# Cross-attention of a decoder layer: the next tile's value projection is issued ahead of its query projection

## The chip, the cores and the metric

The kernel runs on one core of one Trainium2 chip. The metric is the device time of one execution in microseconds (us); lower is better. Given for a kernel is the median of several runs.

## The reference: what is computed

A decoder layer over 16 rows of 128 tokens with 256 features: an RWKV mixing layer in both directions, then a cross-attention on a context of 16 x 128 tokens, then a block with causal attention and a mixture of 8 experts whose weights are quantised in groups of 128. A layer norm stands behind each of the three. The change touches the cross-attention alone:

```
H = 16; D_K = 256 // 16
q = split_heads(x @ Wq + bq)
k = split_heads(ctx @ Wk + bk)
v = split_heads(ctx @ Wv + bv)
scores = einsum('bhqd,bhkd->bhqk', q, k) / sqrt(D_K)
p_attn = softmax(scores, axis=-1)
x = merge_heads(einsum('bhqk,bhkd->bhqd', p_attn, v)) @ Wo + bo
x = layernorm(x_before + x)
```

The expert weights need, for each group of 128 numbers, a largest and a smallest value, a scale and a rounding to 16 levels. The kernel does this for 16 "whole" weight jobs, one in each step of the cross-attention, beside it.

## The kernel before

The program has seven stages, one behind the other: prep, mix, cross, attend, route, experts, finish. Each stage gives each engine its list of instructions, written out by hand; an engine works off its own list in order, and semaphores hold it where it needs another's result. Nothing reorders instructions.

The cross stage (`cross_stage`) has 16 steps, one for each tile n of 128 tokens (step 0 by itself, steps 1 to 12 in a loop of pairs, steps 13 to 15 written out). It is a software pipeline over three tiles. In step n, TensorE (PE) does:

- `scores(j, 1, n)`: the scores of the second half of the heads (L940); `turn_heads` of tile n-1 (L972); `turn_probs(0, n)` (L950); `join` of tile n-1, the output projection (L981), into the PSUM bank `V`
- `front(n+1)`: the transposition of the next tile's x (L913), its keys (L919), its queries (L924, which wait for ScalarE's copy of the turned x, semaphore `x_t_ready`), and its values (L931)
- then four rounds of transposing the quantised weights (`turn_whole`, L993) with the sums over probabilities (`sums`, L962), `turn_probs(1, n)` and `scores(0, n+1)` between them.

The bank `V` is shared by `join` of tile n-1 and by the values of tile n+1. So the values' matmuls wait for `joined_read` (and `v_read`): VectorE (DVE) must have taken the joined rows of tile n-1 out of the bank (`join_stats`, L1202).

DVE does in step n, in this order: `clip` (L1226, waits for `rounded` of ScalarE), `peaks(1, n)` (L1186 and L1189), `steps_of` (L256 to L261), `join_stats(n-1)` (L1202, L752 to L757), `take_values(n+1)` (L1179, waits for `v_ready`), `range_of` (L240, L241), `peaks(0, n+1)`, `normalise(n)` (L1194, L1196), `join_norm(n-1)` (L1209).

ScalarE (ACT) does: `back(n-1)` (L1065), `collect(0, n)` (L1060), `soften(1, n)` (L1055), `take_x(n+1)` (L1041), `round_part` 0 (L1075, two of the weight tiles), `take_qk(n+1)` (L1046 and L1049, waits for `qk_ready` behind the queries), then `take_whole` and `round_part` in turn (L1085, L1075) with `collect(1, n)` between them, until `rounded` and `soften(0, n+1)`.

GpSimd (POOL) builds the whole weights behind the clip (L1151) and spreads the keys (L1133). SyncE's queue loads each weight job and each tile's rows two steps ahead.

Of the kernel before, what the change touches and what calls it, by code (L numbers as in the profile page):

```python
# [27 lines left out]
B, S, D = 16, 128, 256  # L28
TOK = B * S
DC = D // P  # L30
# [729 lines left out]
def cross_stage(k):  # L760
# [8 lines left out]
    nc, t, banks = k.nc, k.t, k.banks  # L769
# [40 lines left out]
    v_ready = k.semaphore("v_ready")  # L810
    v_read = k.semaphore("v_read")
# [19 lines left out]
    TURN, QK, V, SCORES, PROBS_T, HEADS = 0, 1, 2, 3, 5, 7  # L831

    joined_read = k.semaphore("joined_read")
# [67 lines left out]
    def tensor(pe):  # L901
# [5 lines left out]
        def front(j, n, i, begin=False):  # L907

            pe.wait_ge(rows_in[j], 32 * i + 32)
            if not begin:  # L910
                pe.wait_ge(heads_t_ready, n)
            for c in range(DC):
                last = pe.transpose(banks[:, TURN, c * P:(c + 1) * P], x_in[j][:, c * P:(c + 1) * P], k.ident)  # L913
            last.then_inc(x_turned, 1)
            if not begin:
                pe.wait_ge(qk_read, n)
            for m in range(DC):
                for c in range(DC):
                    pe.matmul(banks[:, QK, (DC + m) * P:(DC + m + 1) * P], wk[:, c, m * P:(m + 1) * P],  # L919
                              ctx_t[j][:, c, :], start=(c == 0), stop=(c == DC - 1))  # L920
            pe.wait_ge(x_t_ready, n + 1)
            for m in range(DC):
                for c in range(DC):
                    last = pe.matmul(banks[:, QK, m * P:(m + 1) * P], wq[:, c, m * P:(m + 1) * P],  # L924
                                     x_t[j][:, c, :], start=(c == 0), stop=(c == DC - 1))
            last.then_inc(qk_ready, 1)
            if not begin:
                pe.wait_ge(v_read, n)
                pe.wait_ge(joined_read, n)
            for c in range(DC):  # L930
                last = pe.matmul(banks[:, V, 0:D], ctx_t[j][:, c, :], wv[:, c, :], start=(c == 0), stop=(c == DC - 1))  # L931
            last.then_inc(v_ready, 1)

        def scores(j, h, n, begin=False):
            pe.wait_ge(spread_ready, 2 * n + h + 1)
# [61 lines left out]
        def step(j, n, i, prev, more):  # L997
            def tiles(r):
                turn_whole(j, n, r, min(more, 1))

            scores(j, 1, n)
            if prev:
                turn_heads(1 - j, n - 1, 1)
            turn_probs(0, n)
            if prev:
                join(1 - j, n - 1, 1)
            if more:
                front(1 - j, n + 1, i + 1)
            else:
                pe.wait_ge(qk_read, B)  # L1010
                k.open_attend("pe", pe)
            tiles(0)
            sums(j, 0, n)
            tiles(1)
            turn_probs(1, n)
            if more:
                scores(1 - j, 0, n + 1)
            else:
                pe.wait_ge(scores_read, 2 * B)
                k.open_attend("pe", pe)  # L1020
            tiles(2)
            sums(j, 1, n)
            tiles(3)
            if not more:
                k.open_attend("pe", pe)

        front(0, 0, 0, True)
        scores(0, 0, 0, True)
        in_steps(step, pe)
# [1540 lines left out]
```

## Time and profile before

| what | us |
|---|---|
| median of 3 runs | 1191.3 (1191.14 to 1192.22) |
| the profiled execution, its own time | 1189.91 |
| its span, first to last instruction | 1188.2 |
| cross stage within the span | about 274 to 515 |

A row of the timeline gives the start in us from the span's start, the time taken, the engine, the line, the operation, the tile written and read, and how many instructions are merged in it; in brackets stands the idle time ahead of it and what ended that. Matmuls are pipelined: the next may start before the last one's end. One fp32 matmul of the program is two or more in the trace.

### The profile page before, as it was taken

What the parts mean: (1) busy time and instruction counts of PE and PEld (TensorE: products, weight loads), DVE (VectorE), ACT (ScalarE), POOL (GpSimd) and SP (SyncE); (2) the same over time, 40 slices, a digit from 0 to 9 for tenths busy, and PEclk for the clock granted to TensorE, in tenths of its full rate; (3) what the DMA queues carried; (4) which work ended last, traced back from release to release, by engine and by line L of the source; (5) the groups of instructions that cost most, each with busy time, mean ns of one, the idle gap of its engine ahead of it and who ended that gap; (6) DMA issues with size and microseconds to landing.
All of it is one profiled execution on the core that took longest, in us unless ns stands there. A gap on an engine that the chain in (4) does not pass through costs nothing.

```text
span 1188.2 us, 24715 instructions
## 1 busy us (share of the span) xinstructions
PE 968.9 (82%) x7366; PEld 744.4 (63%) x7367; DVE 959.0 (81%) x2172; ACT 752.0 (63%) x1885; POOL 601.8 (51%) x639
## 2 busy tenths in 40 slices
PE   0495877535999989968999999993799999999991
PEld 0342433324777777745666666662799999999990
DVE  6859999997888888876999998866577777777773
ACT  4864444304888888844666777651477777777773
POOL 2859776853444444421557667751544444434333
PEclk9897988867998899988999999996899999999995
DMA  5860010131333333216122112221122222222224
GB/s 192 346 224 3 1 36 1 35 115 59 117 120 120 120 120 120 90 58 249 38 101 71 59 49 72 67 63 38 32 42 44 37 40 40 39 43 38 40 32 151
DMA packets 53493, 96.77 MB, mean 81 GB/s; under 512 B 9840, under 2 KB 41584, under 8 KB 52928
## 3 DMA queue, kind: packets, MB, share of 16 engines
q1 hardware_dynamic: 45328, 83.35, 20.4%
q0 software_dynamic: 8112, 12.78, 6.2%
q8 instruction: 25, 0.41, 0.1%
q14 instruction: 28, 0.23, 0.1%
HBM read 66.37 MB, written 29.74 MB: 81 GB/s over the span
## 4 chain that ended last, share of the span: by engine, by line
PE 43%; DVE 34%; issue 9%; ACT 5%; POOL 4%; DMA 3%; DVEq 0%; SPq 0%; ACTq 0%; POOLq 0%
PE banks L2166 15%; PE banks L2176 10%; DVE mix_sums L685 4%; DVE carry L672 2%; DVE peak L1186 2%; DVE carry L675 2%; PE banks L1452 2%; DVE probs L1189 2%; DVE whole_stat L241 2%; DVE whole_stat L240 2%; PE banks L1430 1%; PE banks L1475 1%; PE banks L1467 1%; ACT whole_level L1075 1%; PE banks L924 1%
## 5 line engine op out<-in xcount | busy, mean ns | idle before, releaser
L2266 DVE SCALAR_TENSOR_TENSOR expert_gate<-banks,expert_steps,expert_chunk 128x128 f32<-128x128 f32 x546 | 164.8, 346 | 76.8 <-ACT expert_chunk L2226 58.2
L2166 PE MATMUL banks<-expert_parts,levels 128*128 128x128 bf16 x3276 | 196.9, 220 | 1.0 <-ACT expert_parts L2221 1.0
L2166 PEld LDWEIGHTS banks<-expert_parts,levels 128*128 x3276 | 189.0, 98 | 6.9 <-issue 1.2
L2230 ACT ACTIVATE silu<-expert_gate,expert_steps 128x128 f32<-128x128 f32 x273 | 109.6, 402 | 77.9 <-DVE expert_gate L2266 76.0
L488 PE MATMUL banks<-x_turned,w_rkv 128*128 128x512 f32 (+1 forms) x192 | 103.1, 698 | 39.4 <-DVE weight L666 35.4
L2176 PE MATMUL banks<-down,up 128*128 x546 | 134.9, 387 | 0.0
L2337 POOL DMA_INDIRECT summed_d<-expert_y,expert_target x39 | 62.5, 1602 | 126.6 <-ACT expert_y L2236 123.5
L2226 ACT COPY expert_chunk<-banks 128x256 f32<-128x256 f32 x273 | 99.8, 366 | 14.5 <-PE banks L2166 12.9
L1151 POOL TENSOR_TENSOR whole<-whole_level,whole_stat 128x896 bf16<-128x896 f32 x32 | 53.2, 1684 | 102.1 <-DVE whole_level L1226 102.1
L2176 PEld LDWEIGHTS banks<-down,up 128*128 128x128 f32 x546 | 97.6, 190 | 10.4 <-issue 0.4
L488 PEld LDWEIGHTS banks<-x_turned,w_rkv 128*128 128x128 f32 x192 | 42.2, 226 | 97.5 <-issue 92.9
L2273 DVE SCALAR_TENSOR_TENSOR up<-expert_gate,expert_steps,silu 128x128 f32<-128x128 f32 x273 | 95.0, 348 | 8.2 <-ACT silu L2230 8.2
L1075 ACT ACTIVATE whole_level<-whole_raw,whole_stat 128x128 f32<-128x128 f32 x224 | 91.2, 486 | 0.2 <-DVE whole_stat L261 0.2
L585 ACT ACTIVATE weight<-weight 128x1024 f32<-128x1024 f32 x16 | 17.0, 1064 | 70.5 <-DVE weight L666 70.4
L962 PE MATMUL banks<-v_ones,probs_t 128*128 128x17 f32 x512 | 61.1, 261 | 0.0
L962 PEld LDWEIGHTS banks<-v_ones,probs_t 128*128 128x128 f32 x512 | 59.7, 192 | 0.0
L1430 PE MATMUL banks<-attend_w,xn_t 128*128 128x512 f32 x128 | 58.7, 601 | 0.0
L1475 PE MATMUL banks<-attend_w,o_turn 128*128 128x256 f32 x256 | 58.1, 380 | 0.5 <-ACT logits L1591 0.5
L2309 POOL DMA_INDIRECT expert_rows<-normed_d,token x39 | 41.2, 1057 | 31.3 <-POOL token L2306 30.5
L1570 ACT ACTIVATE att_probs<-att_probs,low_peak 128x128 f32<-128x128 f32 x128 | 49.5, 390 | 11.4 <-DVE low_peak L1816 11.3
L1699 POOL TENSOR_TENSOR att_probs<-att_probs,att_share 128x1024 f32<-128x1024 f32 x16 | 30.3, 1896 | 49.8 <-DVE att_share L1820 49.8
L685 DVE RECIPROCAL mix_sums<-gate 128x512 f32<-128x512 f32 x16 | 53.6, 3353 | 0.6
(265 smaller groups left out, 2421.4 us busy)
## 6 DMA issues: line engine op xcount, KB each, us to landing
whole_raw<-in_weight_jobs SPq DMA_DIRECT2D x16, 896.0 KB, 5.3
levels_d<-whole_t SPq DMA_DIRECT2D x16, 448.0 KB, 2.8
levels<-levels_d SPq DMA_DIRECT2D x16, 448.0 KB, 3.9
raw<-in_weight_jobs SPq DMA_DIRECT2D x6, 896.0 KB, 4.9
numbers_d<-turned SPq DMA_DIRECT2D x6, 896.0 KB, 7.4
down<-in_weight_jobs SPq DMA_DIRECT2D x5, 896.0 KB, 7.1
normed_d<-normed_parts SPq DMA_DIRECT2D x16, 192.0 KB, 1.9
attend_w<-numbers_d SPq DMA_DIRECT2D x3, 896.0 KB, 6.6
```

The source lines that it names most:

```text
L488: last = pe.matmul(banks[:, 3 * (u % 2) + m, :], w_rkv[:, kc, col:col + P], x_turned[d][:, kc, bass.ds(g * GT, GT)], start=(kc == 0), stop ...
L685: st.did(dve.reciprocal(sums[p][:, 1, :], gate[u][:, :]))
L962: last = pe.matmul(banks[:, HEADS, head * (XK + 1):(head + 1) * (XK + 1)], probs_t[h][:, 4 * m + a, :], v_ones[j][:, head, :], start=True, ...
L1075: last = act.activation(level[j][:, a, :], raw[j][:, a, :], ACT.Identity, bias=stat[j][:, BIAS, a:a + 1], scale=stat[j][:, INV, a:a + 1])
L1430: last = pe.matmul(banks[:, at[m], :], xn_t[:, c, :], w_qkv[:, c, 512 * m:512 * m + 512], start=(c == 0), stop=(c == DC - 1))
L1475: last = pe.matmul(banks[:, TURN, 0:D], o_turn[:, h, :], w_o[:, h, :], start=(h == 0), stop=(h == QH - 1))
L2166: last = pe.matmul(banks[:, at, (m * DC + c) * ROWS:(m * DC + c + 1) * ROWS], levels[:, bass.ds(expert * (2 * JOB) + (m * JOB + (f * DC + ...
L2176: last = pe.matmul(banks[:, Y + j, 0:D], up[j][:, f, :], down[:, bass.ds(expert * JOB + f * D, D)], start=(f == 0), stop=(f == FC - 1))
L2226: act.copy(chunk[slot(j, f)][:, :, :], halves(at)[:, :, 0, :]).then_inc(chunk_ready, 1)
L2230: act.activation(silu[slot(j, f)][:, :], gate[slot(j, f)][:, 0, :], ACT.Silu, scale=steps[j][:, 0, 0, f:f + 1]).then_inc(silu_ready, 1)
L2266: last = dve.scalar_tensor_tensor(out=gate[slot(j, f)][:, m, :], in0=halves(at)[:, m, 1, :], scalar=steps[j][:, m, 1, f:f + 1], in1=chunk[ ...
L2273: dve.scalar_tensor_tensor(out=up[j][:, f, :], in0=gate[slot(j, f)][:, 1, :], scalar=steps[j][:, 1, 0, f:f + 1], in1=silu[slot(j, f)][:, : ...
```

## The change

In `front` the value projection, with its two waits, is put between the key projection and the queries' wait. The instructions and the waits of each are the same, and only PE's list changes.

```diff
                 for c in range(DC):
                     pe.matmul(banks[:, QK, (DC + m) * P:(DC + m + 1) * P], wk[:, c, m * P:(m + 1) * P],
                               ctx_t[j][:, c, :], start=(c == 0), stop=(c == DC - 1))
+            if not begin:
+                pe.wait_ge(v_read, n)
+                pe.wait_ge(joined_read, n)
+            for c in range(DC):
+                last = pe.matmul(banks[:, V, 0:D], ctx_t[j][:, c, :], wv[:, c, :], start=(c == 0), stop=(c == DC - 1))
+            last.then_inc(v_ready, 1)
             pe.wait_ge(x_t_ready, n + 1)
             for m in range(DC):
                 for c in range(DC):
                     last = pe.matmul(banks[:, QK, m * P:(m + 1) * P], wq[:, c, m * P:(m + 1) * P],
                                      x_t[j][:, c, :], start=(c == 0), stop=(c == DC - 1))
             last.then_inc(qk_ready, 1)
-            if not begin:
-                pe.wait_ge(v_read, n)
-                pe.wait_ge(joined_read, n)
-            for c in range(DC):
-                last = pe.matmul(banks[:, V, 0:D], ctx_t[j][:, c, :], wv[:, c, :], start=(c == 0), stop=(c == DC - 1))
-            last.then_inc(v_ready, 1)
```

On PE, inside the loop over steps, `front` from its keys to the first round of turned weights, with - for before and + for now:

```order
 L919 MATMUL banks<-ctx_t,w_k 128x128 [waits qk_read]
 L919 MATMUL banks<-ctx_t,w_k 128x128 x3
-L921 REGISTER_ALU
-L924 MATMUL banks<-x_t,w_q 128x128 [waits x_t_ready]
-L924 MATMUL banks<-x_t,w_q 128x128 x3
-L931 MATMUL banks<-w_v,ctx_t 128x256 [waits joined_read,v_read]
-L931 MATMUL banks<-w_v,ctx_t 128x256
+L925 MATMUL banks<-w_v,ctx_t 128x256 [waits joined_read,v_read]
+L925 MATMUL banks<-w_v,ctx_t 128x256
+L927 REGISTER_ALU
+L930 MATMUL banks<-x_t,w_q 128x128 [waits x_t_ready]
+L930 MATMUL banks<-x_t,w_q 128x128 x3
```

The four matmuls of the queries now stand behind the wait for `joined_read`, where only the values stood behind it.

On DVE the list is the same before and now. In the loop, the rows that give `joined_read` and take the values are these:

```order
L261 TENSOR_REDUCE whole_stat<-whole_stat 128x14 [waits dve_steps]
L1202 TENSOR_TENSOR joined<-banks,x_bias 128x256 [waits bias_added,joined_ready]
L752 BN_STATS cross_ln<-joined 128x6 [waits joined_read]
L74 REGISTER_ALU
L755 BN_AGGR cross_ln<-cross_ln 128x2 [waits dve_steps]
L74 REGISTER_ALU
L757 TENSOR_SCALAR cross_ln<-cross_ln 128x1 [waits dve_steps]
L1178 REGISTER_ALU
L1179 TENSOR_TENSOR v_ones<-banks,bias_rows 128x16x16 [waits v_ready]
```

Nothing moved here: L1202, which releases `joined_read`, stands behind the peaks and the six small instructions of `steps_of`, as before.

## Rows read from the trace of the kernel before

**Rows 1.** The page, busy time of each engine over the whole span.

```profile
PE 968.9 (82%) x7366; PEld 744.4 (63%) x7367; DVE 959.0 (81%) x2172; ACT 752.0 (63%) x1885; POOL 601.8 (51%) x639
```

**Rows 2.** Busy time by stretch, steps 1 to 14; then clock and DMA.

```profile
core 0: us, PE busy (x) PEld busy (x) DVE busy (x) ACT busy (x) POOL busy (x), PEclk, DMA share, GB/s
290.00:510.00 220.00, 202.54 (x1459) 162.04 (x1458) 190.97 (x316) 193.38 (x449) 96.89 (x89) 0.93 0.33 109
```

**Rows 3.** Waits from 290 to 510 us: total, times, longest.

```profile
DVE v_ones L1179 <- PE banks L931: 16.5, 15, 2.3
...
ACT k_t L1046 <- PE banks L924: 7.6, 15, 0.6
```

**Rows 4.** Timeline of step 9 on PE.

```profile
422.63 1.09 PE L950 MATMUL banks<-consts,probs 128*128 128x128 f32 x8 [0.40 <-ACT probs L1055]
...
424.64 1.06 PE L919 MATMUL banks<-ctx_t,w_k 128*128 128x128 f32 x8
...
426.52 1.16 PE L924 MATMUL banks<-x_t,w_q 128*128 128x128 f32 x8 [0.82 <-ACT x_t L1041]
...
427.51 1.03 PE L931 MATMUL banks<-w_v,ctx_t 128*128 128x256 f32 x4
...
428.38 0.39 PE L993 MATMUL banks<-ident,whole 128*128 128x128 bf16 x4
...
431.55 1.13 PE L940 MATMUL banks<-spread,q_t 64*128 64x512 f32 x4
```

**Rows 5.** Timeline of step 9 on DVE, to the next step's start.

```profile
422.54 1.22 DVE L1186 TENSOR_REDUCE peak<-banks 128x8 f32<-128x1024 f32 x1
...
426.24 0.41 DVE L1202 TENSOR_TENSOR joined<-banks,x_bias 128x256 f32<-128x256 f32 x1
...
428.58 0.42 DVE L1179 TENSOR_TENSOR v_ones<-banks,bias_rows 128x256 f32<-128x256 f32 x1 [0.94 <-PE banks L931]
...
432.77 1.21 DVE L1186 TENSOR_REDUCE peak<-banks 128x8 f32<-128x1024 f32 x1
...
436.20 1.08 DVE L1226 TENSOR_SCALAR whole_level<-whole_level 128x1792 f32<-128x1792 f32 x1
...
437.20 1.22 DVE L1186 TENSOR_REDUCE peak<-banks 128x8 f32<-128x1024 f32 x1
```

**Rows 6.** Timeline of step 9 on ACT.

```profile
426.11 0.35 ACT L1041 COPY x_t<-banks 128x256 f32<-128x256 f32 x1
...
427.71 0.62 ACT L1046 ACTIVATE k_t<-banks,bqk 128x128 f32<-128x128 f32 x2 [0.47 <-PE banks L924]
...
428.80 0.58 ACT L1085 CAST whole_t<-banks 128x512 bf16<-128x512 f32 x1
...
433.53 2.42 ACT L1075 ACTIVATE whole_level<-whole_raw,whole_stat 128x128 f32<-128x128 f32 x6
```

**Rows 7.** Timeline from step 0 into step 1.

```profile
293.85 0.62 ACT L1046 ACTIVATE k_t<-banks,bqk 128x128 f32<-128x128 f32 x2 [0.47 <-PE banks L924]
...
302.16 1.09 DVE L1226 TENSOR_SCALAR whole_level<-whole_level 128x1792 f32<-128x1792 f32 x1 [0.16 <-ACT whole_level L1075]
303.17 1.22 DVE L1186 TENSOR_REDUCE peak<-banks 128x8 f32<-128x1024 f32 x1
```

**Rows 8.** The clip's line alone, steps 1 to 15: durations in ns, starts.

```profile
L1226 DVE TENSOR_SCALAR whole_level<-whole_level x15: 1084/1086/1093, 302.2 to 509.4; 128x1792 f32<-128x1792 f32 x15
```

**Rows 9.** Timeline of step 7, whose first matmuls run slower.

```profile
392.43 1.22 DVE L1186 TENSOR_REDUCE peak<-banks 128x8 f32<-128x1024 f32 x1
...
392.52 1.95 PE L950 MATMUL banks<-consts,probs 128*128 128x128 f32 x8 [0.40 <-ACT probs L1055]
...
393.22 0.35 SPq L212 DMA_DIRECT2D whole_raw<-in_weight_jobs  x1
...
397.10 1.06 PE L924 MATMUL banks<-x_t,w_q 128*128 128x128 f32 x8
...
399.40 2.01 DVE L240 TENSOR_REDUCE whole_stat<-whole_raw 128x14 f32<-128x1792 f32 x1
```

## The prediction

> **What bounds the kernel now.** Over the whole span PE and DVE are about equally busy [rows 1], which says nothing of the stage that is changed. I read the stretch of steps 1 to 14 by itself: of 220.0 us PE works 202.5, ACT 193.4 and DVE 191.0 [rows 2]. Three engines are close to full, so any of them can be the one that sets the length of a step, and only the order of one step tells which. The waits of that stretch have one that fits the change: DVE waits 16.5 us in 15 pieces for the values, L931 [rows 3]. Just as often ACT waits for the queries, L924: 7.6 us [rows 3].
>
> In step 9 I follow DVE from one `peaks(1)` to the next: 422.54 to 437.20, so a step is 14.66 us [rows 5]. DVE has one visible gap in it, 0.94 us ahead of L1179. So the step is DVE's own work plus its wait for the values. The way there goes: peaks(1) at 422.54, ACT's exponential and the copy of x to 426.46, queries on PE at 426.52, values at 427.51, DVE at 428.58 [rows 4 to 6].
>
> There is a second ring, through ACT, nearly as long. From L1046 at 427.71 ACT works without a gap until the end of its last rounding, 433.53 + 2.42 = 435.95 [rows 6]: 8.24 us. That releases the clip, which DVE starts at 436.20 [rows 5]. ACT thus has only 0.25 us to spare. Going from step 0 into step 1 it has none: the clip at 302.16 waited for ACT, and lies 302.16 - 293.85 = 8.31 us behind the L1046 at 293.85; peaks(1) follows 1.01 us later [rows 7].
>
> **The change part by part.** No instruction is added or removed, and no DMA moves. PE's key, query and value matmuls keep their durations. What changes is what each stands behind.
>
> *Values earlier.* They need the keys done and `joined_read`. The keys end at 424.64 + 1.06 = 425.70 [rows 4], but L1202 ends at 426.24 + 0.41 = 426.65 [rows 5]. So PE stands from 425.70 until 426.65, and the values start at about 426.71 (0.06 us from release to start, as between the end of x_t, 426.46, and L924 at 426.52). Before they started at 427.51: 0.80 us earlier. DVE's wait of 0.94 us shrinks to about 0.14.
>
> *Queries later.* They were released by x_t at 426.46. Now they stand behind the wait for `joined_read` and behind the values. The values hold PE for 428.38 - 427.51 = 0.87 us [rows 4], plus 0.10 for a first matmul behind a wait (L924 takes 1.16 here and 1.06 where it did not wait [rows 4, 9]): queries from 426.71 + 0.97 = 427.68 until 428.74, instead of 427.68. ACT starts L1046 at 428.77 instead of 427.71, which is 1.06 us later. Of this 0.19 is the wait for L1202 beyond x_t, and 0.87 the values.
>
> *What is queued behind.* Behind L1046 on ACT stand q_t, all four `take_whole`, the two long roundings and `collect(1)`, without a gap. So `rounded` comes 1.06 us later, at 437.01, and 0.25 of that was spare. The clip can't start before 437.04, where it started at 436.20: 0.84 us late. The 0.80 us that DVE won stands ahead of this wait and is idled away there, or at `peaks(0)`: scores L940 started at 431.55 and ended at 432.68, just ahead of DVE's 432.77 [rows 4, 5], and they stand behind the same block of matmuls on PE, so they don't come earlier.
>
> *The new ring.* From peaks(1): L1202 ends after 426.65 - 422.54 = 4.11; release 0.06; values 0.97; queries 1.06; to L1046 0.03; sum 6.23. From L1046 to the clip 8.24 + 0.03 = 8.27 (8.31 by rows 7); clip to peaks(1) 1.00 [rows 5]. One step is 15.50 us. It closes on itself: L1202 is queued behind peaks(1) on DVE, so a late peaks(1) makes the next `joined_read` late too, and the loss adds up instead of being absorbed.
>
> *Sum.* The wait holds for the fronts of tiles 2 to 15, issued in steps 1 to 14: 14 rings between the first and the last of 15 clips, at 302.2 and 509.4, which is 207.2 us now, 14.80 a step with the steps that ran slower [rows 8]. New: 14 x 15.50 = 217.0 us, 9.8 more. To this comes the slow clock: in step 7, where L950 took 1.95 us and not 1.09 as in step 9 [rows 4, 9], the queries' place (right behind the keys) was only reached at 397.10 - 392.43 = 4.67 us behind peaks(1), not at 4.17 [rows 9]. The values would start there, 0.50 us late. I take 0.7 for all steps, an estimate from this one and a little for others of its kind: 10.5 in all.
>
> *The edges.* Step 0's front (tile 1) has no `joined_read` to wait for; PE idles there for x_t anyhow, the values fit in, and the queries stay where they are. I cost it at nothing; its cover is an idle time like the 0.82 us of step 9 [rows 4], and without it the 0.87 us of the values would be the price. Tile 0's queries come later by the values too, up to twice 0.87 us at the slower pace; DVE's two passes over a weight job, each as long as the 2.01 us of L240 [rows 9], stand ahead of the first peaks and cover it. The late clip of step 15 goes on to POOL's weights, PE's last rounds and the attend stage, one for one: I take all of it, and at the low end 2 us less, for what the next stage may absorb. The next weight job (L212 at 393.22, 0.79 us behind peaks(1), used by L240 at 399.40 [rows 9]) is needed about 0.8 us earlier in the step now; if DVE waits for it there, its own ring (14.66) still has 0.8 us to spare against 15.50.
>
> The sum stands against the profiled execution, 1189.9 us for a span of 1188.2; the median of the runs is 1191.3, 1.4 us higher, and I add the 10.5 us to it: 1201.8 us.
>
> **A rule that speaks the other way.** The trace shows DVE's gap at L1179, 0.94 us in each clean step and 16.5 us over 15 steps, ended by L931 [rows 3, 5]. The Trainium skill, "Perfetto Trace Analysis", section "Optimization Strategy", says to look for the gaps on the engine that one optimises, find what ends them, and make that come sooner. The change does that to the letter. By that rule alone the time would fall by DVE's 0.80 us a step.
>
> **The rivals.**
>
> *Faster: the ACT ring has room (0.04).* If L1046 had at least 1.06 us to spare, each of the 14 steps would lose the 0.80 us of DVE's gap: 11.2 us, 1180 us. This is what the rule of that page would give. For it speaks DVE's gap, the only one it has. It decides where ACT's stretch from L1046 to the clip is under 6.63 us (a step of 14.66 - 0.80 = 13.86, less 6.23 and 1.00), and the rows show 8.24 without a gap [rows 6] and 8.31 with DVE waiting [rows 7].
>
> *No change (0.04).* If the queries did not move: `joined_read` would have to be released 0.97 us before x_t is there, so that the values fit in PE's idle 0.82 us [rows 4]. It comes 0.19 us after x_t in a clean step [rows 5, 6]. 1191.3 us.
>
> *Slower still: the clock (0.07).* PE waits 0.2 us longer ahead of the front and the step is 0.84 us longer with the same work, so PE's busy share falls. The granted clock of the stretch is 0.93 [rows 2]; if the lower level of 1.2 GHz came to the front itself, values and queries would take twice their 1.8 us. If that hits 3 or 4 steps more, 6 us are added: 1208 us. The Trainium skill, "TensorE: Matmul & The Clock Gate", section "HAM oscillation — how this bites in real kernels", warns of repeated idle gaps of PE; which step is hit no row here foretells.
>
> *The ring of ACT, as worked out (0.85).* 1201.8 us, by itself 1199 to 1205.
>
> **How the numbers follow.** The range must hold the ring's case and part of its neighbours. Low end: 14 x 0.70 (a step of 15.50 against the mean of 14.80) is 9.8 already; less 2 for the edges and less 1 for slow steps that it hides gives 1198. High end: 14 x 0.84 = 11.8, the slow clock 1 to 3 more: 1206. A measurement of this kernel tells 0.2% (2.4 us) from no change. Slower: 0.85 + 0.07 = 0.92, to which a small share of odd cases belongs; same 0.04; faster 0.04.
>
> **What would show it.** In the changed profile: the step 15.5 us from L1186 to L1186 in clean steps; PE idle of about 1 us ahead of the values, ended by DVE's L1202; ACT's wait at L1046 for the queries about 1.5 us where it was 0.47, ended by the queries' matmuls; DVE's gap at L1179 down to about 0.1 us, and in its place a wait at the clip L1226 for ACT's whole_level of some 0.4 us or more, or at L1186 for the scores; the clips 217 to 218 us apart from first to last. The prediction is wrong if L1046 starts less than 5.5 us behind peaks(1), or if the clip starts right behind L1209 without a wait: then the ACT ring did not bind.

## The result: slower by 2.3%, nearly three times the forecast

The changed kernel takes 1220.46 us (median of 4 runs, 1211.01 to 1226.19), the kernel before 1191.56 us (4 runs, 1191.14 to 1192.22). The ratio is 1.0232, with a 95% interval of 1.0200 to 1.0264. The sign was forecast, the size was not: 1201.8 us (1198 to 1206) against 1220.5. The profiled execution took 1220.12 us for a span of 1218.4. Ratios here and below are the recorded ones: they leave out runs more than 1.5% above the fastest of the same kernel, and differ a little from the quotient of the medians.

The page of the changed kernel, busy time by engine and the granted clock in 40 slices of the span (tenths of full speed):

```profile
PE 998.1 (82%) x7366; PEld 767.8 (63%) x7367; DVE 963.1 (79%) x2172; ACT 750.7 (62%) x1885; POOL 601.8 (49%) x639
...
PEclk9897988777887778877999999997699999999996
```

PE has the same 7366 matmuls as in [rows 1] and is busy 29 us longer; DVE and ACT hardly change. The clock row shows sevens and eights from slice 10 to slice 19, where the cross stage lies.

Busy time by stretch says it more sharply (columns as in [rows 2]). In the cross stage, the kernel before and then the changed one:

```profile
302.00:505.00 203.00, 187.51 (x1348) 150.48 (x1346) 177.14 (x295) 177.16 (x412) 93.16 (x85) 0.93 0.36 118
302.00:505.00 203.00, 188.60 (x1189) 151.33 (x1188) 163.53 (x256) 156.34 (x364) 81.45 (x74) 0.82 0.32 108
```

The granted clock fell from 0.93 to 0.82, and PE gets 1189 matmuls through where it got 1348. It is busy for as long and has done less: that is a slower clock, not waiting.

The last clip starts at 509.4 us before and at 532.5 us in the changed kernel. The 60 us behind it, before and then changed:

```profile
510.00:570.00 60.00, 45.17 (x214) 30.51 (x213) 43.16 (x101) 25.09 (x73) 17.35 (x15) 0.87 0.42 152
533.00:593.00 60.00, 45.37 (x185) 31.18 (x185) 36.87 (x88) 22.00 (x66) 13.00 (x12) 0.75 0.42 152
```

One step in which the clock held, on the changed kernel's timeline:

```profile
333.64 1.23 DVE L1186 TENSOR_REDUCE peak<-banks 128x8 f32<-128x1024 f32 x1
...
336.19 1.06 PE L919 MATMUL banks<-ctx_t,w_k 128*128 128x128 f32 x8
337.22 0.35 ACT L1041 COPY x_t<-banks 128x256 f32<-128x256 f32 x1
337.35 0.41 DVE L1202 TENSOR_TENSOR joined<-banks,x_bias 128x256 f32<-128x256 f32 x1
...
337.91 1.10 PE L925 MATMUL banks<-w_v,ctx_t 128*128 128x256 f32 x4 [0.66 <-DVE joined L1202]
...
338.85 1.05 PE L930 MATMUL banks<-x_t,w_q 128*128 128x128 f32 x8
339.05 0.42 DVE L1179 TENSOR_TENSOR v_ones<-banks,bias_rows 128x256 f32<-128x256 f32 x1 [0.30 <-PE banks L925]
...
339.94 0.63 ACT L1046 ACTIVATE k_t<-banks,bqk 128x128 f32<-128x128 f32 x2 [1.58 <-PE banks L930]
...
344.09 1.22 DVE L1186 TENSOR_REDUCE peak<-banks 128x8 f32<-128x1024 f32 x1 [0.77 <-PE banks L940]
...
348.11 1.09 DVE L1226 TENSOR_SCALAR whole_level<-whole_level 128x1792 f32<-128x1792 f32 x1 [0.21 <-ACT whole_level L1075]
```

This is the ring as worked out: the values wait for DVE's L1202, DVE's gap at L1179 falls to 0.30 us ([rows 5]: 0.94), ACT's wait at L1046 grows to 1.58 us ([rows 6]: 0.47), and the clip now waits for ACT. L1046 lies 6.30 us behind peaks(1) (forecast 6.23), the clip 8.17 behind L1046 (8.27), the next peaks(1) starts at 349.12: a step of 15.48 us.

And one of the nine steps that follow it, each 17.06 or 17.07 us long from clip to clip but for the first three (17.01 to 17.05):

```profile
451.39 1.22 DVE L1186 TENSOR_REDUCE peak<-banks 128x8 f32<-128x1024 f32 x1
...
451.70 1.96 PE L950 MATMUL banks<-consts,probs 128*128 128x128 f32 x8 [0.28 <-ACT probs L1055]
...
453.45 1.91 PE L981 MATMUL banks<-w_o,heads_t 128*128 128x256 f32 x4
...
455.40 0.42 DVE L1202 TENSOR_TENSOR joined<-banks,x_bias 128x256 f32<-128x256 f32 x1 [0.24 <-PE banks L981]
...
455.59 1.90 PE L919 MATMUL banks<-ctx_t,w_k 128*128 128x128 f32 x8
...
457.30 1.05 PE L925 MATMUL banks<-w_v,ctx_t 128*128 128x256 f32 x4
...
459.28 0.62 ACT L1046 ACTIVATE k_t<-banks,bqk 128x128 f32<-128x128 f32 x2 [2.30 <-PE banks L930]
...
467.45 1.09 DVE L1226 TENSOR_SCALAR whole_level<-whole_level 128x1792 f32<-128x1792 f32 x1 [0.22 <-ACT whole_level L1075]
...
468.46 1.22 DVE L1186 TENSOR_REDUCE peak<-banks 128x8 f32<-128x1024 f32 x1
```

L950, L981 and L919 take 1.96, 1.91 and 1.90 us where [rows 4] have 1.09 and 1.06 for L950 and L919: TensorE ran these at the lower of its two levels, 1.2 instead of 2.4 GHz. It had hardly stood still ahead of them: of its waits from 302 to 505 us none is over 0.7 us. The keys end 6.10 us behind peaks(1), and no longer L1202 (4.43 us) but the keys decide when the values start. L1046 comes 7.89 us behind peaks(1), 1.6 us later than in the clean step, and the ring carries it into the next step, which again begins with slow matmuls in the same place.

**The account.** The span grew by 30.2 us. From the first of the 15 clips to the last it is 230.9 us (301.6 to 532.5) against 207.2 [rows 8]: 23.7. Behind the last clip it is 685.9 us against 678.8: 7.1. Ahead of the first clip 0.6 us were won. Before and changed are one profile each. The second profile of the changed kernel has 686.2 us behind the last clip, those of the other kernels tried have between 680.2 and 683.1, also where they keep the old order, so the 678.8 us of before is a short one, and only some 3 to 6 of the 7.1 us are the changed kernel's own.

### The profile page after: what moved, and what is told of

Read it like the earlier page. It is cut to its first block, busy times and chain, and to the rows that moved or that the text cites. A ratio compares the mean times of both kernels' runs of the same rounds, so it can differ in the third digit from the quotient of the medians.

```text
span 1218.4 us, 24715 instructions
## 1 busy us (share of the span) xinstructions
PE 998.1 (82%) x7366; PEld 767.8 (63%) x7367; DVE 963.1 (79%) x2172; ACT 750.7 (62%) x1885; POOL 601.8 (49%) x639
## 4 chain that ended last, share of the span: by engine, by line
PE 46%; DVE 27%; ACT 11%; issue 9%; POOL 4%; DMA 3%; DVEq 0%; ACTq 0%; POOLq 0%; SPq 0%
PE banks L2166 15%; PE banks L2176 10%; ACT whole_level L1075 4%; DVE mix_sums L685 4%; PE banks L950 2%; ACT whole_t L1085 2%; DVE carry L672 2%; DVE carry L675 2%; PE banks L1452 2%; PE banks L981 2%; PE banks L919 1%; PE banks L1430 1%; PE banks L1467 1%; PE banks L1475 1%; PE banks L1422 1%
## 5 line engine op out<-in xcount | busy, mean ns | idle before, releaser
L962 PE MATMUL banks<-v_ones,probs_t 128*128 128x17 f32 x512 | 63.7, 267 | 1.3
L1570 ACT ACTIVATE att_probs<-att_probs,low_peak 128x128 f32<-128x128 f32 x128 | 49.5, 390 | 11.3 <-DVE low_peak L1816 11.2
```

Source lines behind the costliest of these rows:

```text
L962: last = pe.matmul(banks[:, HEADS, head * (XK + 1):(head + 1) * (XK + 1)], probs_t[h][:, 4 * m + a, :], v_ones[j][:, head, :], start=True, ...
```

## The experiments

Theory A says that the change has two costs: the ring through ACT (15.5 us a step instead of 14.7, some 10 us) and, set off by it, a lower granted clock (the rest). Theory B says that the order alone costs all of it and the clock is no cause. "Before" in the results is the kernel before on the same chip (15 to 19 runs, 1192.2 to 1193.4 us).

**The changed kernel again.**

> The changed kernel once more, for a second profile and more times. Theory A (ring plus clock): the ring of 15.5 us a step is the small part; nine steps of 17.06 us, in which TensorE is granted the lower clock in the first part of each step, are the large part, and how many steps fall into that beat differs from run to run. Then the times spread again over some 10 us (1205 to 1227) and the run's mean granted clock falls as its time rises. Theory B (the order alone): the steps cost what they cost by the waits, 17.06 us, whatever the clock does; then times agree within 3 us and every profile has nine such steps.

1217.64 us (5 runs, 1214.61 to 1220.42), ratio 1.0198 (1.0179 to 1.0217). Its profile repeats the first one: nine steps of 17.01 to 17.07 us, 230.9 us from clip to clip. The times spread over 6 us here and over 15 in the first four runs, where the mean granted clock fell as the time rose (0.902 at 1211.0 us, 0.894 at 1220.1, 0.880 at 1226.2). The spread goes with A, which asked for some 10 us, rather than with B, which allowed 3. But the nine steps came back, as B said, where A expected their number to differ, and in these five runs the time does not follow the mean clock (0.892 at 1215.4 us, 0.889 at 1217.6, 0.894 at 1220.4). So this run does not show which is the cause.

**TensorE's idle time filled, at the front and ahead of turn_heads.** Added work that nothing reads:

```diff
+            if not begin:
+                for _ in range(4):
+                    pe.transpose(banks[:, QK, 0:P], wv[:, 0, 0:P], k.ident)
             if not begin:
                 pe.wait_ge(v_read, n)
                 pe.wait_ge(joined_read, n)
...
             if prev:
+                for _ in range(2):
+                    pe.transpose(banks[:, QK, 0:P], wv[:, 0, 0:P], k.ident)
                 turn_heads(1 - j, n - 1, 1)
```

> The changed kernel with 4 added transpositions of 128x128 on TensorE ahead of the values' wait and 2 ahead of turn_heads, written where the queries or the next keys are written later anyway (work that nothing reads). They fill idle time of TensorE of about 1 us and 0.5 us in a clean step. Theory A: with TensorE busier the lower clock comes less often, the beat of 17.06 us goes, steps are 15.5 to 15.8 us and the time is 1198 to 1208 us. Theory B: the added work changes nothing or adds up to 1.3 us a step in the slow steps: 1220 to 1235 us.

1202.30 us (5 runs, 1201.00 to 1202.44), ratio 1.0071 (1.0057 to 1.0086). More work on TensorE took 15 us away. Of the 14 steps 12 are 15.38 to 15.48 us, and none is over 15.64; 216.7 us from clip to clip. From 302 to 505 us the granted clock is 0.95. B is refuted: order and waits are those of the changed kernel.

**Only at the front, and only elsewhere.** The first has the 4 transpositions at the front alone. The second has none there, 2 ahead of `turn_heads` and these:

```diff
+            for _ in range(4):
+                pe.transpose(banks[:, HEADS, 384:512], wv[:, 0, 0:P], k.ident)
             tiles(2)
```

> The changed kernel with only the 4 added transpositions ahead of the values' wait (the idle time that the change brought to the front). Theory A: that idle time is what tipped the clock; filling it alone gives most of the gain: 1200 to 1208 us. Rival: TensorE's idle time in the rest of the step (ahead of turn_heads and of the third round, where it waits for ACT) is what counts, and the time stays 1212 to 1222 us.

> The changed kernel with 4 added transpositions ahead of the third round of turned weights and 2 ahead of turn_heads, and none at the front. Filling the front alone took the time from about 1218 to 1210 us, front and turn_heads together to 1202 us. If the share of TensorE's work over the whole step decides, this does as well as front and turn_heads together: 1200 to 1206 us. If the idle time at the front is needed as well, 1208 to 1220 us.

Front only: 1210.42 us (4 runs), ratio 1.0135 (1.0112 to 1.0159), steps between 15.46 and 17.43 us; it lies between the two forecasts, and neither theory had it. Elsewhere only: 1200.96 us (6 runs, 1200.75 to 1201.80), ratio 1.0069 (1.0057 to 1.0081). So the idle time that the change itself brought to the front is not what has to be filled; filling it alone gives half. The second shows the ring with no slow clock at all; busy time of its cross stage and its clip's neighbours:

```profile
302.00:505.00 203.00, 182.66 (x1364) 145.36 (x1363) 175.28 (x275) 167.76 (x394) 86.79 (x79) 1.00 0.35 116
```

```profile
430.88 1.10 PE L925 MATMUL banks<-w_v,ctx_t 128*128 128x256 f32 x4 [0.88 <-DVE joined L1206]
...
432.91 0.63 ACT L1050 ACTIVATE k_t<-banks,bqk 128x128 f32<-128x128 f32 x2 [1.58 <-PE banks L930]
...
441.09 1.09 DVE L1230 TENSOR_SCALAR whole_level<-whole_level 128x1792 f32<-128x1792 f32 x1 [0.22 <-ACT whole_level L1079]
```

(Its lines behind the edits stand 4 lower.) The granted clock is 1.00, twelve of the 14 steps are 15.46 or 15.47 us, and the sum is 216.4 us, where 217.0 was forecast. The wait for L1202 is there in each of the 14 steps, 0.86 to 0.89 us. This is the change with its clock effect taken out: 9.2 us in the stage. Before, slow steps are still in the 207.2 us (14 steps of 14.66 us would be 205.2), so clean against clean the ring costs 11.2 us.

**The same filling on the kernel before.**

> Control for the filled wait: the kernel before, with the same 4 added transpositions ahead of the queries' wait for x_t and 2 ahead of turn_heads. Its clock falls for only short stretches already, in some steps. If the added work helps through the clock alone, little is to be won here: steps of 14.6 to 14.8 us and 1188 to 1194 us. If it helped in some other way (an ordering, a wait made shorter), before would gain by it as well, 10 us or more.

1193.80 us (12 runs), ratio 1.0004 (0.9991 to 1.0018): nothing. Seven of its 14 steps are 14.65 to 14.67 us; the other seven are 15.20 to 15.35, longer than forecast, and the 14 take 209.6 us. The transpositions are no gain in themselves.

**The wait alone.** Queries still ahead of values:

```diff
+            if not begin:
+                pe.wait_ge(joined_read, n)
             pe.wait_ge(x_t_ready, n + 1)
             for m in range(DC):
```

> The kernel before, with the wait for joined_read put ahead of the queries, and the values left behind them. Theory A: of the ring's 1.06 us, 0.19 us is this wait and 0.87 us the values; ACT had 0.25 us to spare, so a step stays near 14.7 us and the time within 2 us of before, 1189 to 1194 us. Rival C (the coupling to joined_read is itself what hurts, since a late step makes the next late): most of the loss is there already, 1200 us or more.

1195.68 us (12 runs), ratio 1.0020 (1.0009 to 1.0030), a clean step 14.92 us; A's range ended at 1194. So coupling the queries to `joined_read` costs 0.26 us a step, a little more than A said, since DVE has no slack: its wait at L1179 (here L1181) is 1.20 us instead of 0.94. Rival C, 1200 us or more, falls: most of the 0.8 us a step is the values' own time ahead of the queries.

**A longer step without the change.** Four of ACT's rounding instructions are cut in two; nothing of the order on TensorE is changed:

```diff
             for a in ROUND_PARTS[part]:
-                last = act.activation(level[j][:, a, :], raw[j][:, a, :], ACT.Identity, bias=stat[j][:, BIAS, a:a + 1],
-                                      scale=stat[j][:, INV, a:a + 1])
+                for half in (slice(0, 64), slice(64, P)) if 3 <= a < 7 else (slice(0, P),):
+                    last = act.activation(level[j][:, a, half], raw[j][:, a, half], ACT.Identity,
+                                          bias=stat[j][:, BIAS, a:a + 1], scale=stat[j][:, INV, a:a + 1])
```

> The kernel before, untouched on TensorE, DVE and GpSimd, with 4 of ACT's 14 rounding instructions per step cut into two of 64 columns each, behind its copy of the queries. ACT's ring (14.47 us, with DVE's at 14.66) grows by 4 instructions of an estimated 0.3 us each, to about 15.5 us, as in the changed kernel, with queries ahead of values as before. If the beat of 17.06 us comes from the lower share of TensorE's work in a longer step, some or all steps fall into it here too: 1212 to 1230 us. If it is particular to the new order or to the wait for joined_read, the steps stay at about 15.5 us and the time at 1200 to 1207 us.

1213.78 us (6 runs, 1212.92 to 1225.25), ratio 1.0195 (1.0164 to 1.0226). Shortest steps 15.53 us, as meant; the others up to 17.4, 225.65 us in all, which is 8.2 more than 14 x 15.53; granted clock 0.87 from 302 to 505 us. On its timeline the same matmuls are the slow ones:

```profile
434.19 1.09 PE L950 MATMUL banks<-consts,probs 128*128 128x128 f32 x8 [0.60 <-ACT probs L1055]
435.12 1.03 PE L981 MATMUL banks<-w_o,heads_t 128*128 128x256 f32 x4
...
466.62 1.91 PE L950 MATMUL banks<-consts,probs 128*128 128x128 f32 x8
468.32 1.91 PE L981 MATMUL banks<-w_o,heads_t 128*128 128x256 f32 x4
```

A kernel whose queries stand where they stood, with a step of 15.5 us instead of 14.7, loses 20 us. So a longer step alone is enough to bring the lower clock more often. But the 8.2 us that it loses so are little more than half of the changed kernel's 14.5 (230.9 - 216.4), and the steady beat of 17.06 us did not come. The next runs show that the order has a part in it too.

**The joined rows taken early.** If the values wait for L1202, L1202 can come sooner. DVE takes the joined rows straight behind peaks(1):

```diff
             peaks(1, n)
+            if prev:
+                join_stats(1 - j, n - 1)
             if more:
                 steps_of(1 - j, n + 1, i + 1 if prev else 0)
             if prev:
-                join_stats(1 - j, n - 1)
+                join_rest(1 - j, n - 1)
```

Here `join_stats` is now L1202 alone and `join_rest` the statistics behind it.

> The changed kernel, with DVE taking the joined rows (L1202) straight behind peaks(1), ahead of steps_of; the statistics stay where they were. joined_read then comes about 3.0 us behind peaks(1), before the keys end at 3.16, so the values start without a wait at 3.1 us and the queries at 4.0 us as x_t is ready: L1046 lies 5.1 to 5.2 us behind peaks(1) as before the change, the ACT ring is 14.4 to 14.5 us and DVE no longer waits for the values. Theory A: 1186 to 1190 us, a little faster than before (about 0.2 us in each of 14 steps), if the clock is not worse than before. Theory B, by which values ahead of queries cost by standing there: about 0.87 us a step more than before, 1200 us or more.

> The kernel before (queries ahead of values) with the joined rows taken early on DVE, the other half of the version that holds the changed order. DVE's ring has the same instructions and still waits for the values behind the queries: 14.66 us. Theory A: no change against before, 1190 to 1195 us, so that the gain of the version with both needs the values ahead. Rival: the early taking is what helps, and the clean step is 14.4 us here too: 1188 us or less.

With values ahead: 1201.97 us (8 runs), and these from 1193.99 to 1220.99; ratio of the five fastest 1.0046 (1.0023 to 1.0070). The four steps in which the clock held are 14.34 to 14.36 us, shorter than the 14.66 of before, as A said. But three others are 17.07 and the rest up to 15.55, 213.9 us in all, and the time forecast, 1186 to 1190 us, was missed for the same reason as the first. With queries ahead: 1192.14 us (12 runs), ratio 0.9992 (0.9983 to 1.0001), most frequent short step 14.66 us, 207.6 us in all: taking the rows early does nothing by itself.

Busy time and granted clock of the two, values ahead first, and one of the steps of 17.07 us:

```profile
302.00:505.00 203.00, 188.81 (x1289) 149.45 (x1290) 175.53 (x278) 171.10 (x397) 87.31 (x79) 0.89 0.35 116
302.00:505.00 203.00, 188.56 (x1346) 150.89 (x1346) 176.62 (x296) 176.82 (x410) 92.87 (x85) 0.93 0.35 118
```

```profile
470.90 1.22 DVE L1186 TENSOR_REDUCE peak<-banks 128x8 f32<-128x1024 f32 x1
471.21 1.97 PE L950 MATMUL banks<-consts,probs 128*128 128x128 f32 x8 [0.29 <-ACT probs L1055]
...
475.10 1.90 PE L919 MATMUL banks<-ctx_t,w_k 128*128 128x128 f32 x8
...
478.80 0.62 ACT L1046 ACTIVATE k_t<-banks,bqk 128x128 f32<-128x128 f32 x2 [1.33 <-PE banks L930]
```

This step has no longer clean length to blame: 14.35 us is less than before's 14.66, and still the clock fell, to 0.89, and the beat came, while the same early taking with queries ahead kept 0.93. It is not one profile alone: the mean granted clock over the whole span is 0.888 to 0.910 in the 8 runs with values ahead and 0.914 to 0.925 in the 12 with queries ahead. So the new order lowers the clock even where it makes the clean step no longer. In the slow step L1046 lies 7.90 us behind peaks(1), as in the changed kernel.

**The same, with TensorE's idle time filled** (4 transpositions ahead of `tiles(2)`, 3 ahead of `turn_heads`), run twice, and its control, the same filling on the kernel before.

> Values ahead of queries and the joined rows taken early (clean steps of 14.35 us where the clock held), with 4 added transpositions ahead of the third round of turned weights and 3 ahead of turn_heads, where TensorE idled about 1.1 and 0.9 us a step. Theory A: the beat of 17.07 us at the end of the stage goes, the 14 steps take 201 to 206 us from clip to clip, and the time is 1183 to 1191 us with a small spread. Rival: the added work delays turn_heads or the sums at either clock, and the step is 14.9 us or more: 1194 us or more.

> The fastest version once more (values ahead of queries, joined rows taken early, 7 added transpositions), on the same chip as its control: 1186 to 1190 us, clean steps of 14.35 us.

> Control for the fastest version: the kernel before, order and DVE list untouched, with the same 7 added transpositions (4 ahead of the third round of turned weights, 3 ahead of turn_heads). If the fastest version's gain is the clean step of 14.35 us against 14.66, this one stays at 14.66 us a step or more, and gains only what slow stretches cost before (about 2 us in the stage): 1188 to 1193 us, and it is slower than the fastest version by 2 us or more. If the gain is all the clock's, both have the same time.

1188.10 us (6 runs), ratio 0.9955 (0.9938 to 0.9973), and 1187.84 us (5 runs), ratio 0.9951 (0.9937 to 0.9964): faster than both kernels, and than the one before by 0.4 to 0.5%. In the first profile two steps are still 15.2 and 15.4 us (202.8 us in all). From the second, the clip and the values on DVE:

```profile
431.86 1.09 DVE L1232 TENSOR_SCALAR whole_level<-whole_level 128x1792 f32<-128x1792 f32 x1 [0.22 <-ACT whole_level L1079]
432.87 1.22 DVE L1190 TENSOR_REDUCE peak<-banks 128x8 f32<-128x1024 f32 x1
...
435.35 0.41 DVE L1206 TENSOR_TENSOR joined<-banks,x_bias 128x256 f32<-128x256 f32 x1
...
437.77 0.42 DVE L1183 TENSOR_TENSOR v_ones<-banks,bias_rows 128x256 f32<-128x256 f32 x1
438.03 0.62 ACT L1050 ACTIVATE k_t<-banks,bqk 128x128 f32<-128x128 f32 x2
```

L1050 (before: L1046) lies 5.16 us behind peaks(1), not 6.30; DVE no longer waits for the values from step 1 on; 12 steps are 14.34 to 14.36 us, and the 14 take 200.7 us against 207.2. The control takes 1195.32 us (median of 11 runs, one of which lay at 2028.59 and the others between 1193.45 and 1195.96), ratio 1.0019 (1.0010 to 1.0029), with steps of 14.92 us: the added work holds ACT there, L1050 to the clip 8.75 us instead of 8.27. Its forecast, 1188 to 1193 us, was missed on the slow side, though its granted clock from 302 to 505 us is 0.99. So the gain is not the filling's. That the kernel needs it to keep the gain is seen from its absence above.

## Why the prediction was wrong in size

**The ring: right, to 0.03 us a step.** "One step is 15.50 us": 15.47 in the run without slow clock, 15.48 in the clean step of the changed kernel. Its terms hold: L1046 at 6.30 (6.23), then 8.17 (8.27), then 1.01 (1.00). That DVE's gain would be idled away at the clip or at the scores was right too (0.21 at the clip, 0.77 us ahead of peaks(0) for the scores). "14 x 15.50 = 217.0": 216.4.

**The slow clock: the step that failed.** The sum had "0.7 for all steps", an estimate "from this one and a little for others of its kind", that is from step 7 of before. It measured 230.9 - 216.4 = 14.5 us. Two things in that step were wrong. First, how often the clock falls was taken over from the kernel before as a given. The run with ACT's cut instructions shows that a longer step alone makes it fall more often, and the one with the rows taken early that the new order does so even with a shorter step. Second, the price per hit was too low. In step 7 of before L950 and L981 ran slow (1.95 and 1.89 us) and the keys L919 did not (1.06), which delayed the front by 0.50 us [rows 9]; in the changed kernel the lower level covers L950, L981 and L919 together, the values and queries stand behind all three, and one hit costs 17.07 - 15.48 = 1.6 us.

**The rival "slower still: the clock": the right mechanism, too small and too unlikely.** It had 0.07 and 1208 us, with 3 or 4 hits at the values and queries. It was 9 hits, at the matmuls ahead of them. The Trainium skill, "TensorE: Matmul & The Clock Gate", section on HAM oscillation, warns of a loop in which each turn starts cold; the trace of the changed kernel agrees, with L950 at 1.96 us in one step after another. It does not agree in the cause that the page gives there, a wait for a DMA in each turn: TensorE's waits in this stretch are for ScalarE and VectorE, and the longest is 0.66 us.

**The edges: wrong.** The lateness of the last clip was to be passed on one for one; what stands behind that clip grew by 7.1 us more. In the 60 us behind it the granted clock is 0.75 where it was 0.87. In the runs with a clean cross stage the part behind the last clip is 680.8 us (filled elsewhere) and 682.8 us (the fastest version, second run), against 678.8. But with the old order it is 680.2 to 683.0 us too, so those 2 to 4 us are not shown to come from the change. Which part follows from where the stage's end falls was not tried, and stays open. Step 0 won 0.6 us, costed at nothing.

**The faster and the no-change rival** were rightly refused: DVE's gap did shrink to 0.30 us, and nothing came of it while ACT's stretch stood behind the queries. Only with `joined_read` early, and TensorE's idle time filled, did making the end of the gap come sooner pay, which is where the advice of "Perfetto Trace Analysis" in the Trainium skill held.

What remains open: by what the new order brings the lower clock more often than the old one at the same or a shorter step, and why the two unfilled kernels with values ahead fall into an even beat of 17.06 us and the kernel with ACT's cut instructions does not.

## What to carry to other kernels

Where an instruction is moved ahead of another on an in-order engine, work out every ring that closes through it, with the waits that it brings along; its neighbours' slack decides, and here 0.25 us of slack met 1.06 us. Then look at TensorE's granted clock in the changed kernel before trusting the sum: a loss of 0.8 us a step brought another of 1.0 us a step on average with it (14.5 us over 14 steps). When time is lost that no wait explains, compare the number of matmuls that fit into equal stretches and the granted clock, and fill TensorE's idle time with work that nothing reads as a test.

## What the runs showed of the hardware

Adding six small transpositions a step to TensorE made the kernel 15 to 17 us faster (1217.6 to 1202.3 and 1201.0 us), while the granted clock of the stretch from 302 to 505 us rose from 0.82 to 0.95 and 1.00. Four of them in another place gave only half of that (1210.4 us). Work added to TensorE thus can shorten a kernel, where its clock had fallen; in the kernel before, whose granted clock in that stretch is 0.93, the same work gained nothing (1193.8 against 1193.4 us). And the lower level can fall on the same matmuls in step after step: nine steps in a row of 17.01 to 17.07 us, each with its first matmuls at half speed, came in two profiles alike, with clips 230.87 and 230.90 us apart from first to last. From 302 to 505 us of the first profile TensorE never waited for longer than 0.66 us.
